# The layer-1 edge sort's ranking in four steps per block instead of five, and a third part of the layer-0 edge sums beside the layer-0 experts

## The reference, cut to what matters

```python
loops = jnp.arange(M, dtype=edge_index.dtype)
src = jnp.concatenate([edge_index[0], loops])
dst = jnp.concatenate([edge_index[1], loops])
e = jax.nn.leaky_relu(a_src[src] + a_dst[dst], negative_slope=0.2)
e_max = jax.ops.segment_max(e, dst, num_segments=M)
ee = jnp.exp(e - e_max[dst])
denom = jax.ops.segment_sum(ee, dst, num_segments=M)
alpha = ee / (denom[dst] + 1e-16)
agg = jax.ops.segment_sum(h[src] * alpha[:, :, None], dst, num_segments=M)
...
for ei in range(NUM_EXPERTS):
    g = jnp.where(topk_i == ei, w, 0.0).sum(-1)
    hh = jax.nn.gelu(x @ W1[ei] + b1[ei], approximate=False)
    out = out + g[..., None] * (hh @ W2[ei] + b2[ei])
```

## Time and profile before

| | |
|---|---|
| median of the runs | 3007.59 us (3007.4 to 3023.45) |
| the profiled execution: first to last instruction | 3005.8 us |
| busy over the span | PE 2243.0, PEld 1792.1, DVE 1843.3, ACT 1353.1, POOL 1630.6 us |
| last expert addition on VectorE | at 1444.5 us |
| next stage's first operation on VectorE | at 1530.2 us |
| first gather of ends | at 1534.7 us |
| joined rows used by VectorE | from 1574.1 us |

### The profile page before, as it was taken

The page is one execution under the profiler, slowest core; times in us unless marked ns, Lnnn a source line. Parts: engine busy times, 40 slices in busy tenths (PEclk is TensorE's granted clock), DMA queues, the critical chain, the costliest instruction groups (busy, mean ns, idle before and its releaser), DMA issues. The chain is left out here.

```text
span 3005.8 us, 46144 instructions
## 1 busy us (share of the span) xinstructions
PE 2243.0 (75%) x15376; PEld 1792.1 (60%) x15376; DVE 1843.3 (61%) x4040; ACT 1353.1 (45%) x3268; POOL 1630.6 (54%) x1530
## 2 busy tenths in 40 slices
PE   4487393464599999989622678878774499999998
PEld 4362152453577777877321466666663457999997
DVE  7889556799467887577859566666675830111113
ACT  4368334674312232348706237776672121434343
POOL 0246565466487777778541655777773225344441
PEclk9799696777599999999955788888787599999999
DMA  3240033300333223212542535666662132456335
GB/s 85 65 133 1 19 65 66 68 1 1 63 103 73 63 54 92 65 37 49 135 109 57 128 101 192 209 198 200 206 218 91 37 111 69 139 199 212 127 123 133
DMA packets 186604, 307.78 MB, mean 102 GB/s; under 512 B 90556, under 2 KB 142383, under 8 KB 175698
## 3 DMA queue, kind: packets, MB, share of 16 engines
q1 hardware_dynamic: 109312, 174.45, 19.7%
q0 software_dynamic: 77120, 131.25, 16.1%
HBM read 268.76 MB, written 108.92 MB: 126 GB/s over the span
## 5 line engine op out<-in xcount | busy, mean ns | idle before, releaser
L2378 POOL DMA_INDIRECT ge_near<-gat_src,s_other x448 | 493.3, 1101 | 141.2 <-issue 141.2
L3803 POOL DMA_INDIRECT he_buf<-wh_dram,s_other x400 | 390.3, 976 | 163.1 <-issue 118.5
L983 POOL DMA_INDIRECT pl_table<-s_key,s_other x272 | 305.4, 1123 | 248.7 <-DMA pl_table<-s_key,s_other 172.1
L3298 ACT ACTIVATE x_hT<-bank,x_w 128x128 f32<-128x128 f32 x448 | 164.7, 368 | 262.4 <-PE bank L3240 231.3
L3923 ACT ACTIVATE he_buf<-he_buf,he_e 128x128 f32<-128x128 f32 x800 | 236.4, 386 | 2.5
L3240 PEld LDWEIGHTS bank<-x_xT,x_w 128*128 128x128 f32 x1792 | 208.7, 192 | 2.8
L3240 PE MATMUL bank<-x_xT,x_w 128*128 128x128 f32 x1792 | 208.9, 275 | 0.0
L2769 PE MATMUL bank<-arena 128*125 128x256 f32 x800 | 195.7, 388 | 16.5 <-ACT arena L2777 16.2
L3250 PE MATMUL bank<-x_w,x_hT 128*128 128x256 f32 x896 | 202.5, 379 | 0.0
L4035 DVE SCALAR_TENSOR_TENSOR he_buf<-he_buf,he_cont 128x256 f32<-128x256 f32 x375 | 183.0, 488 | 29.2 <-issue 0.4
L2758 PE MATMUL bank<-XT,arena 128*128 128x250 f32 (+1 forms) x832 | 196.3, 380 | 5.4 <-PEq L73 5.4
(11 more groups left out here) (785 smaller groups left out, 6008.1 us busy)
## 6 DMA issues: line engine op xcount, KB each, us to landing
he_result<-he_buf SPq DMA_DIRECT2D x25, 2080.0 KB, 7.9
XN<-s_a_dram SPq DMA_DIRECT2D x57, 512.0 KB
x_y<-arena SPq DMA_DIRECT2D x48, 224.0 KB
x_x<-zero SPq DMA_DIRECT2D x1, 7196.0 KB, 42.4
x_xs<-x_x SPq DMA_DIRECT2D x56, 128.5 KB, 2.1
ge_near<-gat_src,s_other POOLq DMA_INDIRECT x448
he_buf<-wh_dram,s_other POOLq DMA_INDIRECT x400, 2.8
arena<-x_y SPq DMA_DIRECT2D x2, 2800.0 KB
```

What stands on the lines that cost most here:

```text
L983: pool.indirect_dma_start(out=self.table, out_offset=bass.IndirectOffsetOnAxis(ap=self.goal[:, c:c + 1], axis=0), in_=self.val[:, c:c + 1] ...
L2378: pool.indirect_dma_start(out=G[:, c, 0:HF + H], out_offset=None, in_=m.gat_src, in_offset=bass.IndirectOffsetOnAxis(ap=ed.other[:, c:c + ...
L3298: act.activation(self.hT[u % 2][:, f, :], m.ps[f % 4][:, 0:TS], ACT.Gelu, bias=self.rb1[u % self.B][:, f:f + 1]).then_inc(self.racted, 1)
L3803: pool.indirect_dma_start(out=buf[j][:, c, 0:HF + H], out_offset=None, in_=m.wh_dram, in_offset=bass.IndirectOffsetOnAxis(ap=ed.other[:, t ...
```

## The change

The second sort's ranking takes `PACE` = 4 steps per block: TensorE issues two mask products in each block's last step, ScalarE two masks; VectorE makes the next block's tables (`again`, `turned`) within the block before it. The ring of banks keeps its five uses per block. The ranking then covers steps 38 to 137, the moves 143 to 196 (`end_at` = 197); `vector_finish` stands in step 197, `tensor_end` in 198, the new `vector_keys` (the last line of `vector_finish` by itself) in 199. Nothing of the sort is left behind the last expert step. The single column for the last product moves from bank 2, which the experts use, to bank 6.

The edge sums' parts are now 128 columns each. Part 2 lies among the steps from 184; only part 3 stands behind the loop. SyncE calls `keep(2)` right behind the loop, ahead of X.

```diff
@@ -1296,8 +1297,11 @@
         dve.tensor_tensor(ed.key[:, :], ed.key[:, :], sums, ALU.add)
         dve.drain()
         dve.tensor_copy(self.rsum[:, :], ed.key[:, cols - 1:cols]).then_inc(self.row3, 1)
+
+    def vector_keys(self, dve):
+        key = self.ed.key[:, :]
         dve.wait_ge(self.pre3, 1)
-        dve.tensor_scalar(ed.key[:, :], ed.key[:, :], m.ps[2][:, 0:1], -1.0, ALU.add, ALU.add)
+        dve.tensor_scalar(key, key, self.m.ps[6][:, 511:512], -1.0, ALU.add, ALU.add)
 
 
     def tensor(self, pe):
@@ -1421,6 +1425,7 @@
 
     FIRST = 6
     USES = 5
+    PACE = 4
 
     def __init__(self, m, ed, key_in, other_in, line_in, sb):
         self.placing, self.off = None, 0
@@ -1464,8 +1469,8 @@
         self.ring = [m.ps[0], m.ps[1]]
 
         self.rank_at = self.FIRST + self.nb + 7
-        self.move_at = self.rank_at + self.USES * self.nb + 5
-        self.slots = self.move_at + 2 * (self.nm + 2)
+        self.move_at = self.rank_at + self.PACE * self.nb + 5
+        self.end_at = self.move_at + 2 * (self.nm + 2)
 
         self.loads = Loads(m, tag + "_in")
         self.kb_loaded = [m.sem(f"{tag}_kb_loaded{i}") for i in range(2)]
@@ -1512,7 +1517,7 @@
         t, use = self.block_of(n)
         if n == self.FIRST + self.nb + 1:
             return 2
-        return t + 3 if use == 0 and 0 <= t < self.nb - 3 else None
+        return t + 3 if use == 1 and 0 <= t < self.nb - 3 else None
 
 
     def vector_begin(self, dve):
@@ -1613,32 +1618,34 @@
             self.vector_turned(dve, 0)
         elif a == nb + 1:
             self.vector_totals(dve)
-            self.vector_again(dve, 1)
         elif a == nb + 3:
             self.vector_starts(dve)
-            self.vector_turned(dve, 1)
         elif n == self.rank_at - 2:
             self.vector_within(dve, 0)
         elif n >= self.rank_at:
             t, use = self.block_of(n)
             if t < nb:
-                if use == 2 and t + 1 < nb:
+                if use == 0 and t + 1 < nb:
+                    self.vector_again(dve, t + 1)
+                elif use == 1 and t + 1 < nb:
+                    self.vector_turned(dve, t + 1)
+                elif use == 2 and t + 1 < nb:
                     self.vector_within(dve, t + 1)
                 elif use == 3:
                     self.vector_choose(dve, t)
                     if t + 2 < nb:
                         self.vector_base(dve, t + 2)
-                elif use == 4 and t + 2 < nb:
-                    self.vector_again(dve, t + 2)
-                elif use == 0 and 1 <= t < nb - 1:
-                    self.vector_turned(dve, t + 1)
-            elif n == self.rank_at + self.USES * nb:
+            elif n == self.rank_at + self.PACE * nb:
                 twice = lambda x: x.unsqueeze(2).broadcast_to((128, self.cols, 2))
                 dve.tensor_scalar(self.val2, twice(self.ed.other[:, :]), float(N - 1), -self.MID, ALU.min, ALU.add)
                 self.vector_places(dve)
                 for t in range(2):
                     self.vector_move(dve, t, t)
-            elif n > self.move_at:
+            elif n == self.end_at:
+                self.vector_finish(dve)
+            elif n == self.end_at + 2:
+                self.vector_keys(dve)
+            elif self.move_at < n < self.end_at:
                 t, h = divmod(n - self.move_at, 2)
                 if h == 1:
                     if t + 2 < self.nm:
@@ -1671,11 +1678,14 @@
                     if use == 2:
                         self.tensor_again(pe, t + 1)
                     else:
-                        self.tensor_same(pe, t + 1, use - 3)
-                if use < 4:
-                    self.tensor_rank(pe, t, use)
-            elif n >= self.move_at:
+                        self.tensor_same(pe, t + 1, 0)
+                self.tensor_rank(pe, t, use)
+                if use == 3 and t + 1 < nb:
+                    self.tensor_same(pe, t + 1, 1)
+            elif self.move_at <= n < self.end_at:
                 self.tensor_half(pe, *divmod(n - self.move_at, 2))
+            elif n == self.end_at + 1:
+                self.tensor_end(pe)
 
     def tensor_count(self, pe, t):
         out = self.ring[t // BC][:, t % BC * KB:(t % BC + 1) * KB]
@@ -1774,8 +1784,9 @@
                 if use < 2:
                     self.scalar_mask(act, t, use + 2)
                 elif use > 2 and t + 1 < nb:
-                    self.scalar_mask(act, t + 1, use - 3)
-            elif n == self.rank_at + self.USES * nb:
+                    self.scalar_mask(act, t + 1, 0)
+                    self.scalar_mask(act, t + 1, 1)
+            elif n == self.rank_at + self.PACE * nb:
                 act.wait_ge(self.negated, 1)
                 for h in range(2):
                     self.scalar_half(act, 0, h)
@@ -2317,12 +2328,12 @@
             with Stage(m):
                 layer_norm(m, "ln1", GatNodes(m, m.hg, placing, s, ex))
             s1 = SortBeside(m, next_edges, *next_lists, arena.take)
-            PARTS = ((0, 128), (128, 256), (256, 400), (400, 512))
-            dec = m.sb("ge_dec", [128, 144, H])
+            PARTS = ((0, 128), (128, 256), (256, 384), (384, 512))
+            dec = m.sb("ge_dec", [128, 128, H])
             x_kept = m.dram("x_kept", [P, NT * D])
             x_saved, x_back = Loads(m, "ge_x_saved"), Loads(m, "ge_x_back")
             by = RowsByProducts(m, ed, G, HF + H, s1.rank_at, x_saved, Arena(m.XA, NT * D).take)
-            SPREAD_AT, PART_AT = 64, (86, 150)
+            SPREAD_AT, PART_AT = 64, (86, 150, 184)
             dec_of = lambda q: dec[:, 0:PARTS[q][1] - PARTS[q][0], :]
             rows = [m.sem(f"ge_rows{i}") for i in range(2)]
             e_ready, e_exp, summed = (m.sem("ge_" + x) for x in ("e_ready", "e_exp", "summed"))
@@ -2355,6 +2366,7 @@
                             keep(0)
                         elif q == 44:
                             keep(1)
+                    keep(2)
                     sp.wait_ge(by.taken, by.n)
                     sp.wait_ge(all_by, 1)
                     x_back.nodes(sp, m.X[:, :], x_kept)
@@ -2366,7 +2378,6 @@
                     sp.wait_ge(s1.pre3, 1)
                     ex.reload(sp, 2)
                     ex.reload(sp, 3)
-                    keep(2)
                     keep(3)
 
                 @block.gpsimd
@@ -2471,15 +2482,9 @@
                                 s1.vector_slot(dve, n)
                                 by.vector_slot(dve, n)
                                 n += 1
+                    assert n > s1.end_at + 2
                     dve.drain().then_inc(all_by, 1)
-                    for n in range(n, s1.slots):
-                        s1.vector_slot(dve, n)
-                    s1.vector_finish(dve)
-                    scores(2)
-                    maxima(2)
                     scores(3)
-                    weigh(2)
-                    sums(2, range(H))
                     maxima(3)
                     weigh(3)
                     sums(3, range(H))
@@ -2502,10 +2507,7 @@
                                 s1.tensor_slot(pe, n)
                                 by.tensor_slot(pe, n)
                                 n += 1
-                    for n in range(n, s1.slots):
-                        s1.tensor_slot(pe, n)
                     pe.wait_ge(ex.kept, ex.E * NT)
-                    s1.tensor_end(pe)
 
                 @block.scalar
                 def _(act):
@@ -2536,9 +2538,6 @@
                                 s1.scalar_slot(act, n)
                                 by.scalar_slot(act, n)
                                 n += 1
-                    for n in range(n, s1.slots):
-                        s1.scalar_slot(act, n)
-                    weights(2)
                     weights(3)
 
         def add_nodes(dve, re, rc, we, wc, ws, den):
```

11 lines of the change are left out of this document (6 added, 5 removed).

## The result

The changed kernel is slower by 0.41%: 3019.95 us (20 runs, 3015.94 to 3029.74) against 3008.09 of the kernel before on the same chip (20 runs), a ratio of 1.0041 with an interval of 1.0033 to 1.0050. The forecast of 3034 us was 14 us too high; its sign was right.

A forecast was written before the change was run, and what follows sets the result against it. TensorE sets the steps' pace, SyncE's transfer queue the stage's end. Last addition 1444.9 + 4 + 27 + 16 + 3 = 1494.9, X landed 1512.7, plus 48.8 of transfers: first gather 1561.5, +26.8; median 3034.4 us, range 3011 to 3050.

The forecast's parts named there:

- The chain: Stage's end: last addition, X, then SyncE's queued expert reads and last result set the first end gather, +26.8 us.
- Rival A: SyncE's queue: the result passes the expert reads, VectorE ends the stage; first gather -11, 2997 us; chance 0.07.
- Rival B: SyncE's queue: transfers share, the result lands at 1543; first gather +8, 3016 us; chance 0.05.
- 1444.9 + 4 + 27 + 16 + 3: Expert stream: old end of the last addition plus ranking, moves, two parts and sort's end, giving 1494.9 us.
- four steps per block: Ranking: 25 blocks in 100 steps instead of 125, costing 4 us, bounds -3 to +13.
- 20 more moves: Move steps formerly behind the last expert add to TensorE's pace inside the stream: 20 x 1.35 = 27.0 us.
- part 1 among moves: Edge sums beside the moves: VectorE work beyond its idle time there delays the stream by 8 us.
- part 2: Edge sums newly placed among the late moves: priced at 8 us of delay to the stream.
- the sort's end inside: End of the stream: TensorE waits for VectorE's row sum before its triangular product, 2 to 3 us, taken as 3.
- The lower bound, -3: Ranking at four steps per block: the cost could at best be -3 us, if ends pack better.
- nothing beside ranking: Lower bound for a part's cost: part 1 cost nothing beside ranking, 2.58 against 2.60 us a step.
- rival C: VectorE's parts find cover, no ranking loss: addition at 1475, first gather +7, 3015 us; chance 0.13.

The follow-up runs named there:

- e12: Changed kernel with part 2's result issued right behind X instead of in front of it; 1.0031 of the kernel before.
- e1: Changed kernel with the last part's result stored ahead of the reads of experts 2 and 3; 0.9954 of the kernel before.
- e6: Same edit as e1 on the changed kernel, run where the row gathers stand beside the stage's end; 0.9970 of the kernel before.
- e16: Changed kernel with the last result on ScalarE's queue and the sort's last three steps behind the expert stream; 0.9998 of the kernel before.
- e7: Changed kernel with sort steps from 177 on and part 2 behind the expert stream; 0.9993 of the kernel before.
- e8: Changed kernel with the sort's last three steps (197 to 199) behind the expert stream; 1.0023 of the kernel before.
- e11: Changed kernel with the sums of parts 1 and 2 behind the expert stream; a single execution, last addition +567.1 us after step 30's.
- e4: Changed kernel with part 2 behind the loop again and its result stored behind the experts' reads; 1.0043 of the kernel before.
- e3: Changed kernel with part 1 at step 120 instead of 150 and part 2 at 178 instead of 184; 1.0054 of the kernel before.
- e15: Changed kernel with the last part's result issued on ScalarE's queue instead of SyncE's; 0.9945 of the kernel before.
- e17: Changed kernel with both edits of e1 and e8, row gathers beside the stage's end; 2995.99 us, 0.9948 of the kernel before.
- e13: Changed kernel with both edits of e1 and e8, row gathers ended long before the stage's end; 0.9921 of the kernel before.
- e5: The changed kernel as it is, measured on a second occasion; 1.0055 of the kernel before.
- e18: Kernel of e17 with SyncE also waiting for the row gathers to land before it calls X; 0.9974 of the kernel before.
- e9: Changed kernel with both edits of e1 and e8, row gathers ended long before; 0.9950 of the kernel before.

## Why the prediction was right in its sign and wrong in its size

**The chain was the right one.** The end gathers start when the last result has landed; it stands behind three experts' rows; VectorE's sums end 30 us before the gather, and ending them 22 us sooner still (e12) moves it by 2.5. e1 and e6 show the queue by the order alone, and the packets show the result behind the reads. The 10911 KB took 49.5 us, forecast 48.8. Rival A is out (the gather began 30.2 us after the result was asked for). Rival B, with 28 us for the result, can't be told from the queue by the changed kernel's trace alone (30.2); the 28.1 us of e1, the 7.1 of e6 and the packets' order go with the queue. Turns between transfers do occur, but between two queues (e16).

**What failed is the step that sizes the last addition, "1444.9 + 4 + 27 + 16 + 3".** It gives 1494.9; measured, in the frame of before, 1476.1. Term by term, from the runs, once by the places of the last additions, once by stretches at like clock (the first two rows with the changed kernel's 73.6 us in steps 85 to 102):

| term | forecast | by last additions | by stretches | from |
|---|---|---|---|---|
| four steps per block | +4 | -5.6 | -4.0 | e7 against before, less part 1 |
| 20 more moves | +27.0 | +24.7 | +22.8 | e8 - e7, less part 2 |
| part 1 among moves | +8 | +4 | +3.8 | e12 - e11 |
| part 2 | +8 | +0.6 | +1.3 | e4 |
| the sort's end inside | +3 | +7.3 | +7.2 | after - e8 |
| sum | +50.0 | +31.0 | +31.1 | (+31.2 in the profile) |

*Ranking.* I bounded it by waits that would be added and took VectorE's share of 81% as the sign. The rows after say otherwise: a block alone takes 10.8 to 10.9 us instead of 13.0, where one expert half less accounts for 1.7, so some 0.4 us of each block was not work of TensorE that stays. Over 25 blocks that would be 10; the runs show 4 to 5.6 in the end. Part 0 beside the products takes back 1.7, as it costs 15.0 us over 17 steps instead of 13.3. The lower bound, -3, was drawn too high. That the gain is small waits at the seams between steps is my reading; no run takes it apart. (TensorE was busy 98% to 99% of the time in three of the five windows of before; in the fourth, which the prediction counts with them, it was 97%.)

*Moves.* The forecast priced a move step at 3.08 - 1.73 = 1.35 us. In e7, with nothing of the sort beside them, steps 185 to 197 take 24.04 us, 2.0 each and not 1.73, TensorE busy 21.3 of 24.0. So a move step adds some 1.1 us to what an expert half takes by itself.

*Parts.* The two parts were given one price from the mean of 32 move steps. That mean hid what lay in them. Where part 1 is, VectorE had other work too (57.87 busy of 61.90 us with the part); where part 2 is, it is busy 47% without it. And "nothing beside ranking" was true of the five-step ranking only: e3 shows 6.0 us beside the four-step one.

*The sort's end.* The forecast took 2 to 3 us of waiting. TensorE waits 4.52 for the row sum, and the expert halves queued behind that product come later by as much. And TensorE's clock, no term of the forecast, goes down to 0.50 from 1472.4 to 1479.2, so the first expert half behind takes 3.76 us instead of 1.89: 1.9 us more. Wait and clock are 6.4 of the 7.2 us. In e1, e6 and e15 the clock rose again sooner, and the last four steps take 12.9 us instead of 13.4.

**Two errors of the other sign.** Part 2's result (1536 KB) was seen as taken out of the row, not as put in front of X; X landed 21.7 us after its call instead of 17.0 (16.2 and 16.3 in e12 and e4). And X was called 1.3 us after the last addition's end (1483.32 to 1484.61), not 0.8. The first gather is then 26.8 - 18.8 + 4.7 + 0.5 + 0.7 = +13.9, with 0.7 for the 10911 KB; measured +13.9.

**The forecast that fitted is rival C** (addition at 1475, gather +7, 3015 us). It had 0.13. In the frame of before the addition ended at 1476.1; the gather came 7 us later than C has it, 4.7 of them by part 2's result ahead of X. That C's place for the addition came out is in part luck: it has no loss in the ranking and none at the parts, and measured are a gain of 4.0 and a loss of 5.1, with the moves 4 us cheaper and the sort's end 4 us dearer than in the sum. **The row gathers** ended at 1491.9, in that frame 1484.7, inside the forecast's 1480 to 1490, but "in time for part 3" was wrong: X's read kept them from landing until 1507. That cost nothing, since the result had to queue anyway. It matters in e17, whose first gather stands at +613.0, against +606.2 for the same kernel where the row gathers had ended long before (e13): at most these 7 us are left there.

**Two-way check.** The difference of the last end gather to before, and that of the time (from the ratio), agree to within 3 us over the runs in the two quicker groups: after +13.9 and +12; e5 +13.7 and +17; e6 -8.1 and -9; e7 -3.3 and -2; e8 +7.2 and +7; e16 +0.6 and -1; e17 -16.9 and -16; e18 -6.1 and -8 us. So the one number that the forecast was built on was the right one to follow.

The version to keep is e17: 0.5% under the kernel before (0.9950, 0.9921 and 0.9948 for the same kernel in e9, e13 and e17).

## What to carry to other kernels

When work moves from behind a stage into it, write down what each transfer queue holds at the stage's end and in which order, with the bytes: small results that many wait for go ahead of bulk reads that nobody needs yet, and a second queue does not replace that order once the bulk has been issued: the two queues of e16 took turns by packets, and the small result had the smaller packets. Price a piece of side work by the busy share of its engine in the very steps where it will stand, not by a mean over a stretch. When steps are merged, allow for a gain in the sum: here an engine that was busy 98% gave 4 us back. And where a wait is put in front of TensorE, add what the lower clock costs behind it, here 1.9 us behind a wait of 4.5.
